# Four units of the first group ahead, in eight PSUM banks, and six exponentials moved to the slots in which passes end

## The reference, cut to what matters

```python
xn = (x - mean) / sqrt(var + 1e-5)
# attention, one head of 128, causal
Q, K, V = xn @ Wq, xn @ Wk, xn @ Wv
att = softmax(where(causal, -inf, Q @ K.T * 128**-0.5)) @ V @ Wo
# feed-forward, 4096 features
h = xn @ W1 + b1
R = (cos(theta) * w_real + sin(theta) * w_imag) * w_imag * 0.1
ffn = relu(h + R * sin(theta + 0.1 * h)) @ W2 + b2
out = x + att + ffn
```

## Time and profile before

| | |
|---|---|
| median of 3 runs | 1016.36 us (1015.97 to 1016.71) |
| the profiled execution's own time | 1016.68 us |
| its span, slowest core (core 1) | 1014.9 us |
| spans of the 8 cores | 1012.8 to 1014.9 us |
| TensorE busy | 98% |
| VectorE, ScalarE, GpSimd busy | 59%, 39%, 9% |

### The profile page before, as it was taken

The page is one execution under the profiler, slowest core; times in us unless marked ns, Lnnn a source line. Parts: engine busy times, 40 slices in busy tenths (PEclk is TensorE's granted clock), DMA queues, the critical chain, the costliest instruction groups (busy, mean ns, idle before and its releaser), DMA issues.

```text
span 1014.9 us, 21165 instructions; the slowest of 8 cores (1012.8 to 1014.9 us)
## 1 busy us (share of the span) xinstructions
PE 998.7 (98%) x7387; PEld 687.7 (68%) x7387; DVE 601.1 (59%) x1512; ACT 396.7 (39%) x741; POOL 86.9 (9%) x154
## 2 busy tenths in 40 slices
PE   7999899999999999999999999999999999999998
PEld 7666567676666766667676666766667676676665
DVE  5666766656566665565555555666566656655544
ACT  3355433433444344442433444334443434444321
POOL 5700110100001000010100001010010100000000
PEclk9999999999999999999999999999999999999999
DMA  9999962633335342353523324242342533414421
GB/s 176 175 174 177 174 129 64 124 83 92 59 78 114 89 111 53 91 111 86 117 74 75 64 72 112 82 103 60 99 86 75 129 88 70 93 43 103 94 52 43
DMA packets 89656, 98.85 MB, mean 97 GB/s; under 512 B 62032, under 2 KB 62160, under 8 KB 89552
## 3 DMA queue, kind: packets, MB, share of 16 engines
q1 hardware_dynamic: 76448, 61.82, 23.3%
q0 software_dynamic: 12384, 34.61, 21.2%
q10 hardware_dynamic: 720, 1.08, 0.3%
HBM read 84.02 MB, written 16.78 MB: 99 GB/s over the span
## 4 chain that ended last, share of the span: by engine, by line
PE 90%; DMA 4%; DVE 2%; POOL 1%; issue 1%; ACT 0%; DVEq 0%; SPq 0%; ACTq 0%; POOLq 0%
PE psO L594 41%; PE psW L513 41%; DMA W_sb<-w 3%; PE psA L349 3%; PE psA L466 1%; PE psA L397 1%; PE psA L369 1%; PE psO L573 1%; DVE X L552 1%; POOL W_sb L209 1%; DMA X<-x 1%; DVE bn L291 0%; DVE bn L289 0%; POOL W_sb L202 0%; DVE u L526 0%
## 5 line engine op out<-in xcount | busy, mean ns | idle before, releaser
L513 PE MATMUL psW<-xn,W_sb 128*128 128x256 bf16 x4064 | 518.9, 273 | 5.9 <-DVE u L526 4.3
L594 PE MATMUL psO<-W_sb,rb 128*128 128x512 bf16 x2048 | 505.0, 379 | 2.3 <-DMA W_sb<-w 1.6
L513 PEld LDWEIGHTS psW<-xn,W_sb 128*128 128x128 bf16 x4064 | 394.7, 98 | 136.9 <-issue 9.5
L521 ACT ACTIVATE ss<-psW,ph_sb 128x256 bf16<-128x256 f32 x508 | 237.8, 474 | 567.4 <-PE psW L513 373.0
L526 DVE SCALAR_TENSOR_TENSOR u<-ss,Rp_sb,psW 128x256 f32<-128x256 bf16 x508 | 243.4, 479 | 303.8 <-ACT ss L521 303.2
L594 PEld LDWEIGHTS psO<-W_sb,rb 128*128 128x128 bf16 x2048 | 198.7, 98 | 170.7 <-issue 4.9
L543 DVE TENSOR_SCALAR rb<-u,fp_sb 128x256 bf16<-128x256 f32 x506 | 177.6, 351 | 47.9 <-DVE u L526 22.8
L552 DVE TENSOR_TENSOR X<-psO,X 128x512 f32<-128x512 f32 x96 | 59.9, 681 | 2.5 <-PE psO L594 2.4
L295 POOL TENSOR_SCALAR rs<-mv 128x1 f32<-128x1 f32 x32 | 7.9, 246 | 561.6 <-DVE mv L293 517.8
L719 POOL DMA_DIRECT2D X<-b2rep x32 | 29.5, 922 | 307.8 <-DMA X<-x 293.4
L408 DVE TENSOR_SCALAR_CACHE_REDUCE lg<-psA 128x512 f32<-128x512 f32 (+2 forms) x80 | 48.3, 603 | 0.0
(11 more groups left out here) (60 smaller groups left out, 277.5 us busy)
## 6 DMA issues: line engine op xcount, KB each, us to landing
X<-x SPq DMA_DIRECT2D x56, 512.0 KB, 5.4
X<-b2rep POOLq DMA_DIRECT2D x32, 512.0 KB, 5.7
out<-X SPq DMA_DIRECT2D x64, 256.0 KB, 3.3
W_sb<-w POOLq DMA_DIRECT2D x40, 256.0 KB, 27.5
W_sb<-w POOLq DMA_DIRECT2D x12, 512.0 KB, 70.2
X<-x ACTq DMA_DIRECT2D x4, 256.0 KB, 7.7
X<-x SPq DMA_DIRECT2D x4, 256.0 KB, 7.3
Wqkv_sb<-wqkv POOLq DMA_DIRECT2D x1, 768.0 KB, 22.6
```

The source lines that it names most:

```text
L513: fn = lambda e, k=k: e.matmul(bank[:, 0:GT], w1_block(c, k), xg[:, k * GT:(k + 1) * GT], start=(k == 0), stop=(k == NCD - 1), skip_group_ ...
L521: t_sin[u] = act.mark(lambda e: e.activation(sines, bank[:, 0:GT], AF.Sin, scale=0.1, bias=ph_sb[:, c:c + 1]))
L594: fn = lambda e, i=i, tt=tt, h=h, u=u, c=c: e.matmul(psO[i][:], rb_of[u][:, tt * 128:(tt + 1) * 128], W2_sb[:, c * D + h * 512:c * D + (h ...
```

## The change

- `HEAD` 2 to 4 and `NWIDE` 6 to 8: the first four units are group 0's, then units 4, 6, 8, ... are group 1's features 0, 1, 2, ... and units 5, 7, 9, ... group 0's features 4, 5, 6, ...; the first eight units have a bank each, the last two of them in `psA`. The multiply-adds and relus of the first four are queued after the transposes of tiles 2 and 3, which move to slot 3.
- `phases` comes right after `angles`; the first load of W1 waits for the whole of tile 0 of x. Loads of weights are reordered. The addition of epsilon in `ln_stats` is VectorE's.
- From J = 6 on the causal mask is not added on TensorE: VectorE adds it in an operation of its own with a maximum of its own.
- `expo` of tiles 0 to 5 moves from slots 23, 27, 34, 38, 43, 54 to 25, 31, 37, 43, 50, 57, and the VectorE part of it (`scale`) to the slot after. The lag is no longer lowered after it. A triple below slot 62 is emitted 8 slots after the pass's last turn instead of 7: in slots 13, 19, 25, 31, 37, 43, 50, 57 (before: 12, 18, 24, 29, 36, 40, 48, 56). From slot 62 on the turns stand as before.

```diff
-HEAD = 2
-NWIDE = 6
+VMASK = 6
+HEAD = 4
+NWIDE = 8
...
-            pool.after(t)
-            t = pool.mark(lambda e: e.tensor_scalar(
+            dve.after(t)
+            t = dve.mark(lambda e: e.tensor_scalar(
                 rs[i][:, 0:1], mv[i][:, 1:2], LNEPS, None, ALU.add))
...
+            on_pe = last and J < VMASK
...
-            if last:
+            if on_pe:
                 pe.do(fn)
                 fn = lambda e: e.matmul(
                     psA[b][:, w - 128:w], idn_sb[:], mask_sb[:], start=False,
...
+            seen = w - 128 if last and not on_pe else w
...
+            if last and not on_pe:
+                top += 1
+                own = lg[:, si * 512 + seen:si * 512 + w]
+                dve.after(t_mask)
+                t = dve.mark(lambda e: e.tensor_tensor(
+                    own, psA[b][:, seen:w], mask_sb[:], ALU.add))
+                dve.after(t)
+                t = dve.mark(lambda e: e.tensor_reduce(
+                    mx[:, top:top + 1], own, AX.X, ALU.max))
...
+            if J >= 2 * XBAR - 2:
+                scale(J)
+
+        def scale(J):
...
-        wide = psW + psO
+        wide = psW + psO + psA
...
+            if u >= HEAD:
+                f1_out(u, bank, sines)
+            else:
+                held.append((u, bank, sines))
...
-                2: (21, 22, 23, 25, 30, 31, 33), 3: (12, 13, 15, 30, 20, 31, 33),
+                2: (21, 22, 23, 27, 29, 33, 34), 3: (12, 13, 15, 30, 20, 31, 33),
...
             at(e0, lambda: expo(J))
+            at(e0 + 1, lambda: scale(J))
             at(p0, lambda: weighted(J))
-
-            for slot, less in ((2, 2), (3, 2), (4, 1), (5, 1)):
-                lag[e0 + slot] = usual_lag(e0 + slot) - less
...
-        pool.after(t_sc)
-        for p in range(4):
+        t_rp, t_ph = phases(t_sc)
+        pool.after(t_half[0], t_x[0])
+        for p in range(3):
             load_w1(p)
         stats(0)
-        load_w1(4)
-        t_rp, t_ph = phases(t_sc)
+        load_w1(3)
         stats(1)
-        load_w1(5)
-        load_w1(6)
+        for p in range(4, 7):
+            load_w1(p)
...
         stats(2)
+        load_w2(0)
         stats(3)
...
-        load_all((2, 0), (2, 1), (2, 2), (2, 3), (2, 4), (2, 5), (1, 7), (1, 8), (1, 9),
-                 (1, 10))
+        load_all((2, 1), (1, 7), (2, 2), (2, 3), (2, 4), (2, 5), (1, 8), (1, 9), (1, 10),
+                 (1, 11))
         t_wqkv = l_wqkv.start(pool, lambda e: e.dma_start(Wqkv_sb[:], wqkv))
-        load_all((1, 11), (2, 6), (2, 7), (1, 12), (2, 8), (2, 9), (2, 10), (2, 11),
-                 (1, 13), (1, 14))
+        load_all((1, 12), (2, 6), (2, 7), (1, 13), (2, 8), (2, 9), (2, 10), (2, 11),
+                 (1, 14), (1, 15), (1, 16), (1, 17), (1, 18), (2, 12), (2, 13), (1, 19),
+                 (2, 14), (2, 15), (2, 16), (2, 17), (1, 20))
         t_wo = l_wo.start(pool, lambda e: e.dma_start(Wo_sb[:], wo))
...
-        at(0, lambda: idle_work(8))
-        for tile in (2, 3):
-            at(1, lambda tile=tile: ln_transpose(tile, *tms[tile], norms[tile], act))
-            at(1, lambda: idle_work(16))
+        def second_tiles():
+            ln_transpose(2, *tms[2], norms[2], act)
+            idle_work(10)
+            ln_transpose(3, *tms[3], norms[3], dve)
+            idle_work(10)
+            for h in held:
+                f1_out(*h)
+
+        at(HEAD - 1, second_tiles)
...
-        for g, slot in ((0, 20), (1, 28), (2, 37)):
+        for g, slot in ((0, 20), (1, 28), (2, 41)):
...
-        plan_tile(0, 22, 23, 27, 29)
-        plan_tile(1, 24, 27, 31, 32)
-        plan_tile(2, 33, 34, 38, 39)
-        plan_tile(3, 35, 38, 42, 43)
-        plan_tile(4, 40, 43, 47, 50)
-        plan_tile(5, 48, 54, 58, 62)
+        plan_tile(0, 22, 25, 29, 31)
+        plan_tile(1, 27, 31, 35, 37)
+        plan_tile(2, 34, 37, 41, 42)
+        plan_tile(3, 39, 43, 47, 49)
+        plan_tile(4, 46, 50, 54, 56)
+        plan_tile(5, 53, 57, 61, 63)
...
-                if len(ns) > 1 and slot < end + min(3, lag.get(slot, LAG)):
+                if len(ns) > 1 and slot < end + (8 if slot < 62 else
+                                                 min(3, lag.get(slot, LAG))):
```

More of the change, by code:

```diff
@@ L398, in logits @@
                 psA[b][:, 0:w], Q_fm[:, half * 128:(half + 1) * 128],
-                K_fm[:, si * 512:si * 512 + w], start=True, stop=not last,
+                K_fm[:, si * 512:si * 512 + w], start=True, stop=not on_pe,
                 skip_group_check=True)
-            if last:
+            if on_pe:
                 pe.do(fn)
@@ L407, in logits @@
             dve.after(t, state["exp"])
-            t = dve.mark(lambda e: e.tensor_scalar(
-                lg[:, si * 512:si * 512 + w], psA[b][:, 0:w], 1.0, None,
-                ALU.mult, ALU.max, accum_out=mx[:, si:si + 1]))
+            seen = w - 128 if last and not on_pe else w
+            if seen:
+                t = dve.mark(lambda e: e.tensor_scalar(
+                    lg[:, si * 512:si * 512 + seen], psA[b][:, 0:seen], 1.0, None,
+                    ALU.mult, ALU.max, accum_out=mx[:, si:si + 1]))
+            top = si if seen else si - 1
+            if last and not on_pe:
[7 more added lines that the diff above has]
+                    mx[:, top:top + 1], own, AX.X, ALU.max))
             bank_free[b] = t
@@ L414, in logits @@
                 t_max[J] = dve.mark(lambda e: e.tensor_reduce(
-                    mx[:, 4:5], mx[:, 0:si + 1], AX.X, ALU.max, negate=True))
+                    mx[:, 5:6], mx[:, 0:top + 1], AX.X, ALU.max, negate=True))
         def expo(J):
@@ L421, in expo @@
             state["exp"] = t_exp[J] = act.mark(lambda e: e.activation(
-                pr[:, 0:n], lg[:, 0:n], AF.Exp, bias=mx[:, 4:5],
+                pr[:, 0:n], lg[:, 0:n], AF.Exp, bias=mx[:, 5:6],
                 accum_out=sm[J % 2][:, 0:1]))
             act.do(lambda e: e.preload_act_table_set("trig_and_small"))
+            if J >= 2 * XBAR - 2:
+                scale(J)
+        def scale(J):
+            n = (J % 16 + 1) * 128
             dve.after(t_exp[J])
@@ L493, in build_nc @@
                  for g, a, b in passes for c in range(a, b)]
-        wide = psW + psO
+        wide = psW + psO + psA
         wide_ss = [ss[0][:], ss[1][:]] + [
-            lg[:, 1536 + 128 * i:1664 + 128 * i].bitcast(BF16) for i in range(NWIDE - 2)]
+            lg[:, 256 + 128 * i:384 + 128 * i].bitcast(BF16) for i in range(NWIDE - 2)]
         rb_free = [(i, None) for i in range(NRB)]
@@ L511, in f1 @@
             pe.after(t_w1[PIECE_OF[c]], t_xn[g, 0], t_xn[g, 1], t_stt.get(old))
+            if NWIDE - 2 <= u < NWIDE:
+                pe.after(bank_free[u - NWIDE + 2])
             for k in range(NCD):
@@ L522, in f1, with f1_out @@
                 sines, bank[:, 0:GT], AF.Sin, scale=0.1, bias=ph_sb[:, c:c + 1]))
+            if u >= HEAD:
+                f1_out(u, bank, sines)
+            else:
+                held.append((u, bank, sines))
+        held = []
+        def f1_out(u, bank, sines):
+            c = units[u][1]
             if u >= 1:
@@ L528, in f1 @@
                 bank[:, 0:GT], ALU.mult, ALU.add))
+            if NWIDE - 2 <= u < NWIDE:
+                bank_free[u - NWIDE + 2] = t_stt[u]
         def on_act(u):
@@ L757, in load_all @@
                 (load_w1 if which == 1 else load_w2)(p)
-        load_all((2, 0), (2, 1), (2, 2), (2, 3), (2, 4), (2, 5), (1, 7), (1, 8), (1, 9),
-                 (1, 10))
+        load_all((2, 1), (1, 7), (2, 2), (2, 3), (2, 4), (2, 5), (1, 8), (1, 9), (1, 10),
+                 (1, 11))
         t_wqkv = l_wqkv.start(pool, lambda e: e.dma_start(Wqkv_sb[:], wqkv))
-        load_all((1, 11), (2, 6), (2, 7), (1, 12), (2, 8), (2, 9), (2, 10), (2, 11),
-                 (1, 13), (1, 14))
+        load_all((1, 12), (2, 6), (2, 7), (1, 13), (2, 8), (2, 9), (2, 10), (2, 11),
+                 (1, 14), (1, 15), (1, 16), (1, 17), (1, 18), (2, 12), (2, 13), (1, 19),
+                 (2, 14), (2, 15), (2, 16), (2, 17), (1, 20))
         t_wo = l_wo.start(pool, lambda e: e.dma_start(Wo_sb[:], wo))
[L765 to L768, removed]
-        at(0, lambda: idle_work(8))
-        for tile in (2, 3):
-            at(1, lambda tile=tile: ln_transpose(tile, *tms[tile], norms[tile], act))
-            at(1, lambda: idle_work(16))
+        load_all((1, 21), (1, 22), (2, 18), (2, 19), (2, 20), (1, 23), (2, 21), (2, 22),
+                 (1, 24), (1, 25), (2, 23), (2, 24), (2, 25))
+        def second_tiles():
[6 more added lines that the diff above has]
+        at(HEAD - 1, second_tiles)
         at(16, lambda: load_x(4, 4, t_stt[14]))
```

## The result

Over 17 runs the changed kernel's median is 1018.37 us, against 1016.71 us for the kernel before: ratio 1.0015, 95% interval 1.0008 to 1.0022. The forecast was 1018.6. What counts as a difference was set at 0.2%, so this is "within 0.2%", though the interval lies above 1. The medians are over all 17 executions; the ratio leaves out the three of each kernel in which one die ran slower than the other throughout. The profiled execution took 1018.57 us; its slowest core spans 1017.0.

A forecast was written before the change was run, and what follows sets the result against it. The stream of weights bounds before unit 25, TensorE's work behind it. 1.4 + 2.6 + 0.2 - 1.4 - 6.5 + 6.0 = +2.3 us on 1016.68 gives 1019.0; the median lies 0.3 lower, 1018.6; range 1013.1 to 1021.

The forecast's parts named there:

- The forecast's sum: Unit 25 to the end: 950.6 us before, +2.6 triple, +0.2 logits, -1.4 mask, -6.5 old late starts, +6.0 new ones.
- The late starts: TensorE after unit 25, to 160 us: the old 6.5 us of waits go, new ones of 6.0 us come (1.5 to 8).
- half hidden: Rival, chance 0.25: the waits behind the table loads and exponential overlap, leaving 3.5 us of late starts; time 1016.1 us.
- hidden in full: Rival, chance 0.20: the triple covers the exponential, VectorE catches up, 1.5 us of late starts are left; time 1014.1 us.
- the wait of `probs_t` of tile 4: Slot 54: TensorE waits behind VectorE's statistics of tile 7 and the logits of slot 53, 1.2 us.
- The mask: 26 mask matmuls at 0.055 us leave TensorE, -1.4 us; VectorE's added 5 to 18 us are hidden and cost nothing.
- The landing of W1's piece 14: Before unit 25: the piece lands at 65.7 us as now, TensorE idles some 3 us, unit 25 starts 1.4 us later.
- The same bytes: Weights' queue ahead of W1's piece 14: old and new order hold the same pieces, only permuted, so its landing stays.
- The first load's later issue: Start: the first load waits for tile 0 of x, 8.35 against 6.06 us; taken as 0, ends -0.5 and +2.3 us.
- the third rival: Chance 0.12: the wait before unit 25 halves TensorE's clock for 3.3 us, costing 1.7 us; time 1020.3 us.
- each time anew: Quoted skill rule: every DMA wait of a few us halves TensorE's clock again; by it all eight cores would pay here.

## Why the prediction was right, and where it was not

**What bounds the kernel, and what follows unit 25: right.** The forecast's sum has 951.5 us from unit 25 to the end (950.6 + 2.6 + 0.2 - 1.4 - 6.5 + 6.0). Core 1, whose clock held there, takes 1013.9 - 62.64 = 951.3. Core 0 takes 1017.0 - 63.90 = 953.1, 1.6 more.

**The late starts: right in size and in place.** 6.0 were forecast, 5.76 measured, and each of the named waits is there. That half of them come from the LayerNorm work behind the exponential is shown by moving it (5.76 to 2.85). So *half hidden* and *hidden in full* are out: the waits do not overlap. One term is only half right: the wait of `probs_t` of tile 4 (0.9, for `lg`) was VectorE's, as forecast, but behind it stands one of 1.0 for a bank that ScalarE's copy `pT` frees. It shows once tile 7's statistics are moved, and went when tile 5's logits came a slot earlier.

**The mask: right in sign.** -1.4 was forecast, the mask alone gave -1.0, with an interval that reaches from -2.0 to -0.1.

**The landing of W1's piece 14: mis-sized.** The step let it land at 65.7, as on the slowest core before; "before unit 25, which starts near 65.7" and "wrong if unit 25 starts before 64.5" hung on it. It started at 63.90 on core 0 and at 63.36 as a mean, so by its own sign this step was wrong. GpSimd's issue on core 1 and its time to landing, which answer to the earlier trace rows:
```profile
27.70 0.84 POOL L203 DMA_DIRECT2D W_sb<-w  x1
DMA to landing us min/median/max: 34.7/34.7/34.7
```
It lands at 62.4, 3.3 us sooner than on the same core before; over the cores the mean goes from 64.65 to 62.96. "The same bytes" ahead was right: by the landing GpSimd's queue has moved 8.14 MB before and 8.15 after (means of the cores). What the step left out is SP's queue. The load of x for tile 5 comes with unit 24, and SP issues it at 60.9 instead of 58.0 (means). By the landing of piece 14, 0.32 MB of it had moved before, and nothing after. SP's issue on core 1:
```profile
60.56 0.33 SPq L182 DMA_DIRECT2D X<-x  x1
```
The DMA view of core 1 (packets, MB, share of the engines; q0 is the queue of the weights, q1 that of x), before from 63 to 65 us, then after from 61 to 63:
```profile
q0 software_dynamic: 96, 0.18, 65.8%
q1 hardware_dynamic: 49, 0.20, 30.2%
...
q0 software_dynamic: 196, 0.36, 108.1%
```
While x is carried, the weights' queue moves half as much. The size of it can be read from the run with the mask alone, which has the old loads and the old start: by 61 us its queue of weights had moved as much as the changed kernel's (7.81 MB, means of the cores), SP issued x at 57.6, and piece 14 landed at 64.25, 1.3 us later. The other 0.4 of the 1.7 us is that the profiled execution of the kernel before was already behind at 61 us (7.72 MB). No run moved that load alone. The first load's later issue cost nothing, as forecast: the first piece lands at 14.84 instead of 15.15 (means).

**The clock: the third rival came true on half the cores, at its price.** 1.7 us were forecast, 4.21 - 2.59 = 1.6 measured on core 0. It was given a chance of 0.12, and it made up what the earlier landing had saved. On the slowest core the two errors are -1.8 and +1.6, and that is why the total is right to 0.2 us: this is luck, as nothing ties the one to the other. Without this fall the span of that core would have been near 1015.4, and core 7, which paid its fall at unit 13, the slowest with 1016.3. The rival's own time, 1020.3, was missed, since it had the late landing in it. Against the rule of the Trainium skill, "TensorE: Matmul & The Clock Gate", section "HAM oscillation", as the prediction quoted it: a fall came after a wait for a DMA on all eight cores somewhere, which speaks for the rule, but "each time anew" does not hold, and before unit 25 four cores paid and not all eight. Core 0 sat idle 2.37 us before unit 13 at full clock and 2.39 before unit 25 with a fall.

**Where the change went.** The four units ahead and eight banks work in the stretch that is bound by the stream of weights, and come out at +0.7 us, which can't be told from nothing; the mask at -1.0; the exponentials in the slots of the triples at +1.9. That last idea is good only in company: it takes the triple from in front of unit 25, where it filled a wait for a weight, and puts LayerNorm work behind the exponential. With the weight's place in the queue, the LayerNorm work of three tiles and one slot of logits mended, the same kernel goes from 1.0015 to 0.9954.

## What to carry to other kernels

When a block of work is moved behind a point that waits for a transfer, two things change: the wait that it used to fill opens, and the transfer's own place in the queue is now wrong; move the transfer too. To hide a long operation on another engine, count what the bound engine has between the two points in the new order, unit by unit: one turn of 0.9 us behind each of five exponentials made most of the difference between 1016.10 and 1012.21. And when a transfer's landing is taken over from another trace, look at every queue that shares the DMA engines with it, not only at its own.

## What the runs showed of the hardware

In the profiled execution of the changed kernel the granted clock fell to 0.50 for 3.4 us (on core 7 for 6.8 us) behind single waits of 2.0 to 3.4 us, and not at every such wait. At unit 13 cores 1, 5, 6 and 7 lost it, with waits of 2.33 to 3.36 us, and cores 0, 2, 3 and 4 didn't, with 2.37 to 2.87; at unit 25 it was the other four. A core that had lost time to it once reached the next wait late enough to keep its clock there, so no core fell at both waits, and the program paid for the worst core. This does not hold for every execution: in two others the slowest core has a mean clock of 0.996 and a span of 1017.3 and 1017.4.

Filling the gaps with idle matmuls kept the clock on every core of the profiled execution (spans 1014.3 to 1015.6) but moved the median by no more than half a microsecond, and the mean span of a core over the 14 and 12 executions not at all (1015.2 in both).

Two queues share what the DMA engines carry: on core 1 before, the weights' queue moved 0.18 MB in the 2 us in which the load of x moved 0.20 MB beside it, and 0.36 MB in 2 us after, without it. The bytes of x began to move 4.1 us after SP's issue before and 3.7 after (means of the cores), so a load can slow another queue well after its own issue.
